# Where the layer norm statistics of z are computed: VectorE's batch-norm instructions or ScalarE's accumulators

## What is computed

```python
def layer_norm(y):
    m = jnp.mean(y, -1, keepdims=True)
    v = jnp.var(y, -1, keepdims=True)
    return ln_gamma * (y - m) * jax.lax.rsqrt(v + EPS) + ln_beta
...
def fp_step(y_prev):
    x_tilde = (x - y_prev) @ W_mix.T + y_prev
    bc = _shift1(y_prev) @ W_bc.T
    Bt = bc_normalize(B0 + bc[..., :D_STATE])
    Ct = bc_normalize(C0 + bc[..., D_STATE:])
    y = _selective_scan(x_tilde, delta, A, Bt, Ct, D)
    return layer_norm(y)
y0 = jnp.zeros_like(x)
y_star = jax.lax.fori_loop(0, FP_ITERS, lambda i, y: y + STEP * (fp_step(y) - y), y0)
y = fp_step(y_star)
```

## Time and profile before

| | us |
|---|---|
| median of 3 runs | 10860.2 (10859.1 to 10865.62) |
| profiled execution | 10862.61 |
| its span, first to last instruction | 10860.6 |
| one turn of the loop (root to root, 297.29 to 343.86) | 46.57 |

### The profile page before, as it was taken

The page is one execution under the profiler, slowest core; times in us unless marked ns, Lnnn a source line. Parts: engine busy times, 40 slices in busy tenths (PEclk is TensorE's granted clock), DMA queues, the critical chain, the costliest instruction groups (busy, mean ns, idle before and its releaser), DMA issues.

```text
span 10860.6 us, 255134 instructions
## 1 busy us (share of the span) xinstructions
PE 9541.8 (88%) x87052; PEld 6371.4 (59%) x87052; DVE 9046.9 (83%) x16798; ACT 6987.6 (64%) x14760; POOL 6114.8 (56%) x4900
## 2 busy tenths in 40 slices
PE   7988889888898888988889888898888988889888
PEld 4656656566565665656656566565665656656566
DVE  6978869789697886978879788797887978879788
ACT  5766657566575665756657566675666756667576
POOL 1936719367292672926729276292762927629276
PEclk9999999999999999999999999999999999999999
DMA  0000000000000000000000000000000000000000
GB/s 20 0 3 1 2 2 0 3 1 2 2 0 3 1 2 2 0 3 1 2 3 0 3 1 2 2 0 3 1 2 2 0 3 1 2 2 0 3 1 3
DMA packets 648318, 23.40 MB, mean 2 GB/s; under 512 B 629169, under 2 KB 646978, under 8 KB 647362
## 3 DMA queue, kind: packets, MB, share of 16 engines
q1 hardware_dynamic: 647746, 16.11, 3.5%
HBM read 9.40 MB, written 4.19 MB: 1 GB/s over the span
## 4 chain that ended last, share of the span: by engine, by line
DVE 32%; PE 24%; issue 17%; POOL 15%; ACT 7%; DMA 2%; DVEq 2%; POOLq 1%; SPq 0%; ACTq 0%
DVE work L1483 17%; POOL work L1575 14%; DVE work L1473 6%; PE ps L563 4%; PE ps L568 4%; PE ps L578 3%; ACT da L976 2%; PE ps L511 2%; DMA hend<-work 2%; PE ps L499 2%; POOL skip_u L1558 1%; DVE yT L1455 1%; ACT da L895 1%; DVE stats L1121 1%; PE ps L476 1%
## 5 line engine op out<-in xcount | busy, mean ns | idle before, releaser
L1575 POOL TENSOR_TENSOR work<-work,crep 128x512 f32<-128x512 f32 x4608 | 5764.0, 1275 | 912.4 <-DVE work L1473 549.6
L1006 ACT ACTIVATE scan_in<-du,bcn 128x256 f32<-128x256 f32 x8704 | 3630.1, 497 | 0.0
L746 PE MATMUL ps<-w_ident,scan_in 128*128 128x128 f32 x18432 | 2718.7, 283 | 416.3 <-ACT da L976 146.7
L1483 DVE TENSOR_TENSOR_SCAN work<-da,hend,ps 128x256 f32<-128x256 f32 x4608 | 3035.4, 724 | 19.8 <-PE ps L746 6.8
L746 PEld LDWEIGHTS ps<-w_ident,scan_in 128*128 128x128 f32 x18432 | 2056.8, 144 | 1343.6 <-issue 840.5
L1473 DVE TENSOR_TENSOR_SCAN work<-da,ps 128x512 f32<-128x512 f32 x2304 | 2656.4, 1201 | 50.6 <-PE ps L746 35.3
L1558 POOL TENSOR_TENSOR skip_u<-u_sb,w_skip 128x512 f32<-128x512 f32 x288 | 374.4, 1300 | 3754.0 <-ACT u_sb L990 3754.0
L735 PE MATMUL ps<-work,w_sel 128*32 128x256 f32 x18432 | 1475.5, 392 | 222.1 <-POOL work L1575 210.0
L929 ACT ACTIVATE work<-ps,w_gate_b 128x512 f32<-128x512 f32 x512 | 352.0, 687 | 897.2 <-PE ps L563 896.6
L1228 DVE TENSOR_REDUCE smax<-ps 128x1 f32<-128x512 f32 x1024 | 661.3, 686 | 199.7 <-PE ps L476 195.8
L735 PEld LDWEIGHTS ps<-work,w_sel 128*32 128x32 f32 x18432 | 362.8, 108 | 727.5 <-POOL work L1575 467.7
(11 more groups left out here) (180 smaller groups left out, 11878.0 us busy)
## 6 DMA issues: line engine op xcount, KB each, us to landing
hend<-work SPq DMA_DIRECT2D x2304, 1.0 KB, 1.8
x_in<-in_x SPq DMA_DIRECT2D x17, 256.0 KB, 2.8
out<-work SPq DMA_DIRECT2D x16, 256.0 KB
gate_w<-in_gate_w SPq DMA_DIRECT2D x1, 1024.0 KB, 4.7
up_w<-in_up_w SPq DMA_DIRECT2D x1, 1024.0 KB, 6.8
down_w<-in_down_w SPq DMA_DIRECT2D x1, 1024.0 KB, 8.8
w_w_in<-in_w_in SPq DMA_DIRECT2D x1, 256.0 KB
w_w_zy<-in_w_zy SPq DMA_DIRECT2D x1, 256.0 KB
```

The source lines that it names most:

```text
L746: mm = eng.transpose(ps[:, RING[p % 4], c:c + P], scan_in[:, m, tb, 2 * j + s].rearrange("p k c -> p (k c)"), ident[:])
L1006: ins = eng.activation(scan_in[:, m, tb, :, k, :], du[:, hf, tb, :].rearrange("p (e c) -> p e c", c=GC), ACT.Copy, scale=bcn[:, hf, tb, 0, ...
L1483: ins = eng.tensor_tensor_scan(hst[:, p % NHID, half], da[:, 1, 2 * p + s, :], ps[:, RING[p % 4], half], hend[:, 2 * p + s:2 * p + s + 1], ...
L1575: eng.tensor_tensor(prod[:, p % PROD, :].rearrange("p (s t) -> p s t", s=2), hst[:, p % NHID, :].rearrange("p (s t) -> p s t", s=2), crep[ ...
```

## The change

The statistics move to ACT. `back_mean` is two copies of z scaled by −1/256 whose accumulators write −mean (`z_mean`); it stands behind the fill of group 1. `back_square` is two squares of z with that −mean as bias, whose accumulators write the sum of squared deviations (`z_square`); it stands behind `back_keep`. The root then takes 1/256 of it as scale. The elements that the four instructions write go to vn's storage and are not used. DVE keeps the reciprocal. nmr is made on ACT by two copies of one column, at the head of `back_v`, which waits for them.

```diff
-DVE_VAR, DVE_NORM, DVE_Y, DVE_BC, DVE_BCN, DVE_DU = 3, 4, 6, 8, 9, 10
+DVE_NORM, DVE_Y, DVE_BC, DVE_BCN, DVE_DU = 4, 6, 8, 9, 10
...
+            def back_mean(at, hf, kb):
+
+                eng.wait_ge(z_done.sem, z_done.count(at, kb + 1))
+                for tb in range(HB):
+                    ins = eng.activation(vn[:, tb, :], half5[:, tb, :], ACT.Copy, scale=-1.0 / DI,
+                                         accum_out=z_mean[:, tb:tb + 1])
+                ins.then_inc(zmean.sem, zmean.up(at))
+
+            def back_square(at, hf, kb):
+
+                eng.wait_ge(zmean.sem, zmean.count(at, kb + 1))
+                for tb in range(HB):
+                    ins = eng.activation(vn[:, tb, :], half5[:, tb, :], ACT.Square,
+                                         bias=z_mean[:, tb:tb + 1], accum_out=z_square[:, tb:tb + 1])
+                ins.then_inc(zvar.sem, zvar.up(at))
+
             def back_root(at, hf, kb):
                 eng.wait_ge(zvar.sem, zvar.count(at, kb + 1))
-                eng.activation(std[:, 0:HB], meanvar[:, 0:HB, 1], ACT.Sqrt, bias=eps[:]
+                eng.activation(std[:, 0:HB], z_square[:], ACT.Sqrt, bias=eps[:], scale=1.0 / DI
                     ).then_inc(zstd.sem, zstd.up(at))
 
             def back_v(at, hf, kb):
+                eng.wait_ge(zrstd.sem, zrstd.count(at, kb + 1))
+                for tb in range(HB):
+                    ins = eng.activation(nmr[:, tb:tb + 1], z_mean[:, tb:tb + 1], ACT.Copy,
+                                         scale=rstd[:, tb:tb + 1])
+                ins.then_inc(znmr.sem, znmr.up(at))
                 eng.wait_ge(znmr.sem, znmr.count(at, kb + 1))
...
                 fill(at, hf, 1, 1).then_inc(filled.sem, filled.up(at))
+                back_mean(at, other, kb)
                 if kf is not None:
                     back_keep(at, other, kb)
+                back_square(at, other, kb)
                 back_root(at, other, kb)
...
-            def back_var(at, hf, kb):
-                eng.wait_ge(z_done.sem, z_done.count(at, kb + 1))
-                moments(at, half5, zvar, HB)
-
             def back_norm(at, hf, kb):
                 eng.wait_ge(zstd.sem, zstd.count(at, kb + 1))
-                eng.reciprocal(rstd[:, 0:HB], std[:, 0:HB]).then_inc(vchain.sem, vchain.up(at))
-                eng.wait_ge(vchain.sem, vchain.last(at))
-                eng.scalar_tensor_tensor(
-                    out=nmr[:, 0:HB], in0=meanvar[:, 0:HB, 0], scalar=-1.0, in1=rstd[:, 0:HB],
-                    op0=ALU.mult, op1=ALU.mult).then_inc(znmr.sem, znmr.up(at))
+                eng.reciprocal(rstd[:, 0:HB], std[:, 0:HB]).then_inc(zrstd.sem, zrstd.up(at))
...
                     if follows:
-                        if p == DVE_VAR:
-                            back_var(at, other, kb)
                         if p == DVE_NORM:
```

More of the change, by code:

```diff
@@ L154, in hybrid_kernel @@
         nmr = sb("nmr", [P, TB])
+        z_mean = sb("z_mean", [P, HB])
+        z_square = sb("z_square", [P, HB])
         da = sb("da", [P, 2, NG, TH])
@@ L246, in hybrid_kernel @@
         stored = signal("stored", behind=1, unit=16)
-        vchain = signal("vchain", 46, 8, 20)
+        vchain = signal("vchain", 46, 4, 16)
         class Norm:
@@ L346, in hybrid_kernel @@
         zstd = signal("zstd", *back)
+        zmean = signal("zmean", *back)
+        zrstd = signal("zrstd", *back)
         znmr = signal("znmr", *back)
@@ L1102, in _ @@
                 back_sum(at, 1, 1)
+                back_mean(at, 1, 1)
+                back_square(at, 1, 1)
                 back_root(at, 1, 1)
@@ L1546, in _ @@
                 scan_unit(at, 1, 0, 0, None)
-                back_var(at, 1, 1)
                 back_norm(at, 1, 1)
```

## The result

The changed kernel takes **11305.35 us** (median of 4 executions, 11277.84 to 11354.75). The kernel before, run beside it, takes 10862.91 (10859.1 to 10869.28). The ratio is **1.0412, with a 95% interval of 1.0394 to 1.0429**. Forecast were 11298 us. The profiled execution took 11306.69 us, with a span of 11304.6: 444.0 more than the span before, where the prediction's sum was 438.

A forecast was written before the change was run, and what follows sets the result against it. DVE was taken to bound the loop, with little slack in the chain through ACT. 16 × (8 × 3.13 + 0.7 + 1.65) = 438 us more gave 11298 us against the median; forecast itself 11184 to 11415, range 11070 to 11530.

The forecast's parts named there:

- The bound and the place: In the loop: DVE is the bound; the chain through ACT to y has only 0.34 and 0.67 us of slack.
- r: On ACT: extra time per accumulating instruction for writing its sum out, four in a unit; taken as 0.2 us, between 0 and 0.4.
- the mean pair: In the chain through ACT: two copies with accumulators, 0.56 + 0.40 us.
- square to root: In the chain through ACT: two squares with accumulators until the root begins, 0.90 + 0.40 + 0.02 us.
- Nothing in the rest of the unit can give the time back: DVE has no idle time there, so y's delay of 1.72 and 1.41 us, 3.13 a turn, is paid in full.
- Scan 4: On DVE after the statistics: it could start only 0.37 us sooner, since PE transposes its input.
- what would show: Signs in the profile after: a 49.7 us turn, DVE idle before the reciprocal and before y, ACT near 40 us a turn.
- Rival 4: TensorE's clock falls as PE idles before vn: 550 us more in all, 11850 us; chance 0.03.
- Outside the loop: In each of 16 batches: 0.7 us more in the last unit and 1.65 us more in the tail.
- rival 2: The accumulators are free, r near 0: about 11070 to 11150 us; chance 0.17.
- Rival 1: DVE is the bound, so what leaves it is won: 2.0 us a turn, 256 us, 10604 us; chance 0.03.
- Rival 3: The accumulator read drains ACT, r of 0.35 or more: 11470 to 11550 us; chance 0.13.

The follow-up runs named there:

- Dummy4: The kernel before, statistics still on DVE, with four spare ACT instructions without accumulators in every unit of the loop: 10913.8 us, ratio 1.0048.
- keep_early: The changed kernel with ytmp issued on ACT before the copy of the sums instead of between mean and square: 11021.5 us, ratio 1.0139 to before.
- dummy8: The kernel before, statistics still on DVE, with eight spare ACT instructions without accumulators in every unit of the loop: 11457.6 us, ratio 1.0547.
- both: The changed kernel with ytmp before the copy of the sums and nmr back on DVE as one two-column product: 10900.8 us, ratio 1.0030 to before.
- split_ts: The changed kernel with ytmp early, nmr on DVE by two one-column tensor_scalar instructions, and two of four group 2 fills behind vn: 10763.3 us, ratio 0.9906 to before.
- warm: The changed kernel with PE's transposes for scan input 7 issued three times, in the pause before vn: 11184.4 us, ratio 1.0290 to before.
- nmr_dve: The changed kernel with nmr back on DVE as one two-column product behind the reciprocal: 11029.6 us, ratio 1.0149 to before.
- before_ts: The kernel before, statistics on DVE, with nmr by two one-column tensor_scalar instructions instead of one with two SBUF inputs: 10804.1 us, ratio 0.9932.

## Why the prediction was right, and where it was not

**The bound and the place: right.** The forecast rested on the slack of the chain through ACT, not on the idle time in sum. The waits appeared where it put them, at the reciprocal (put to ACT's root) and before y (put to PE's transposes of vn), and y's delay of 2.12 us makes up the longer turn, 2.06. DVE's busy time fell to 43.7 us a turn (about 43 forecast) and ACT's rose to 39.2 (about 40). Dummy4 and keep_early move the turn through the length of the chain alone, dummy8 through the chain and the clock that falls with it.

**r: over-sized.** The step "I take 0.2, by the row for nrm" took the length of a small instruction for what it keeps the engine from doing. The read is as long as that row, 0.20 us, but for the most part hidden: 0.07 is left. Over eight accumulators that is 1.0 of the 3.13 us a turn. The other terms (ytmp 0.80, root to fill 0.21, fills 1.59, nmr 0.50) came within 0.03; the mean pair was 0.71 (0.96 forecast) and square to root 1.04 (1.32). The loop's chain was thus forecast at 16 × 8 × 3.13 = 401 us, and cost 250.8.

**"Nothing in the rest of the unit can give the time back": right.** The delays in the two units, 2.12 us, are in the turn to within 0.06.

**Scan 4: not as forecast.** "DVE could start scan 4 only 0.37 us sooner": it was 0.15 us in the unit of half 0, and 0.37 in the other (5.73 where it was 6.10). The idle time of 0.91 us before it was not on the list of what would show. It costs nothing here, since the waits behind it swallow it; in `both` and split_ts (0.91 and 0.92 us in the unit of half 0) most of what the statistics leave is lost there.

**Rival 4, the clock: wrongly dismissed.** It got a chance of 0.03 with "busy 43 of 49.7 is far from half". The share over a turn was the wrong thing to look at, as the share over the span is for the bound. PE is busy 43.0 of 48.8 us and has one pause of 1.67 us in each unit, its others being 0.54 or less, and behind it the clock fell in 76 turns, for 176.4 us. With the pause cut to 0.80 (warm) it never fell, nor with 1.15 (nmr_dve) and 1.03 (keep_early), where PE had nothing more to do. It was a part of the time, not the 550 us of the rival, but as large as two thirds of the chain's own cost. The Trainium skill ("TensorE: Matmul & The Clock Gate", the part on the clock gate) has the hardware set the clock by how busy TensorE has been lately; the trace agrees as far as it goes: the clock fell within 1.1 us behind a pause, though not behind every pause of that length.

**Outside the loop: over-sized.** 16 × (0.7 + 1.65) = 38 us were forecast, 16.8 measured. The tail's chain is 681.27 − 678.30 = 2.97 us long, against 1.81: 1.16 more, not 1.65, and r makes up the difference (four times 0.13 us too much). Its two ends in the trace after:

```profile
678.30 0.38 ACT L1039 ACTIVATE yscT<-ps 128x256 f32<-128x256 f32 x1 [1.32 <-PE ps L721]
...
681.27 1.02 ACT L1064 ACTIVATE yscT<-ps,nmr,rstd 128x256 f32<-128x256 f32 x2
```

In the unit behind the loop scan 8 is 0.80 us later in the median (12.88 against 12.08 us into the unit; forecast 0.7). Both together would be 31 us, 15 more than measured. The clock is the likely place of the rest: outside the loop after has 834 us at the lower clock, before 940. Of the 16 units behind the loop 3 have such a stretch in after and 7 in before, and summed up they are 0.7 us shorter in after, although at a clock of 1.00 one lasts 22.02 against 21.37. That 106 us less at the lower clock are worth the missing 15 is argued from these rows, not shown by a run. Across the kernels the part outside the loop varies between 4888 and 4960 us; before_ts, at the lower end, has 851 us at the lower clock in it, and keep_early, at the upper, 1086.

So the forecast of +438 against a measured +444 is errors that cancel: 150 us too much for the chain and 21 for what is outside, 176 us too little for the clock. That it came so close is luck. Without the clock's part the time would be about 11130, inside the range, but below the 11184 to 11415 of the forecast itself and among the times of rival 2. **Rival 1** (what leaves DVE is won) stays refuted for this order of the work, and gets its due in split_ts: with a chain of 2.91 us, well below the 3.70 that the prediction named, the turn falls below that of every kernel with the statistics on DVE; at 3.71 (`both`) it is only level. **Rival 3**, a draining read, is settled by the reads. **Rival 2** was nearer than its chance of 0.17 says: the reads are not free, but r of 0.06 to 0.08 lies below the 0.1 to 0.3 of the forecast.

What stays open: why the clock falls in some units behind the loop and not in others, and why the number of drops differs between executions of the same kernel. After has a spread of 77 us, and its slowest execution has the lowest mean clock (0.937) and its fastest the highest (0.944), where the kernel before, run beside it, spreads over 10 us. In the profiled execution 9 batches have a drop of 6.8 us in each turn but the first, and the other 7 have one or three of 3.4 us, so that a few batches more or less of the first kind would make such a spread. That it comes from the drops is argued from these clocks, not shown turn by turn.

## What to carry to other kernels

Before work is moved to an engine with idle time, follow the chain that the moved result belongs to, through every engine, and find the slack at its end: here 0.34 and 0.67 us, against 11.6 us of idle time in sum; what stays within it is nearly free, what exceeds it is paid in full and then by whoever stands behind the wait. When the work is moved all the same, take out of the chain what only stands in it by order (here ytmp and two fills), and give the small product a form that does not wait; here the move then pays, by 0.3 to 0.7 us in a turn of 46. And count what a new wait does to the matmul engine's clock: a pause that is short beside the turn can slow the work behind it.

## What was not expected of the hardware

- The accumulator's sum is written by an instruction of its own behind each ACTIVATE. It lasts 197 and 204 ns in the mean behind the two forms, but adds under 0.1 us from start to start, since it begins before its ACTIVATE ends and the next one begins before it ends. An instruction that reads the sum at once costs some 0.15 us more of waiting (keep_early). The groups of after:

```profile
L1047 ACT ACTIVATE yscT<-ps,z_mean 128x256 f32<-128x256 f32 x576 | 265.4, 469 | 1.0
...
L1047 ACT ACTIVATION_READ_ACCUMULATOR yscT<-ps,z_mean 128x1 f32 x576 | 117.2, 204 | 0.0
...
L1059 ACT ACTIVATE nmr<-z_mean,rstd 128x1 f32<-128x1 f32 x576 | 133.9, 279 | 3.7 <-DVE rstd L1469 3.7
```

- A copy of one column with a per-partition scale takes 279 ns on ACT, over half as long as one of 256 columns with a bias (469).
- A two-column product of two SBUF inputs on DVE took from 482 to 2127 ns beside GpSimd's work and 160 in the tails, where GpSimd is idle, while two one-column products with a per-partition factor took 203 to 216 ns each. That exchange alone is worth 0.68% of the kernel (before_ts).
- The granted clock fell behind pauses of 1.67 us, one in each unit, in a loop whose PE is busy for 88% of the time, for 3.4 or 6.8 us, in 76 of 128 turns; with the pause at 1.98 us (dummy8) in 127, with 1.15, 1.03 and 0.80 us in none.
